# Half of the stack fetches issued by GpSimd, two transfers for the maxima, maxima dealt from the third quad on

## The chip, the cores and the metric

The kernel runs on one core of one Trainium2 chip. The metric is the device time of one execution in microseconds (us). The median of three runs of the kernel before is 1971.94 us (1971.53 to 1973.84).

## The reference

The input `x` has 16 batches of 512 tokens with 256 features. The reference is two residual blocks, each between two layer norms:

```
x = x + layernorm(attention(layernorm(x)))
x = x + layernorm(ffn(layernorm(x)))
```

The attention has 16 heads of 16 features. The 512 tokens are 8 blocks of 64; the first and the last block see all tokens, the others see the first block, the last block and their neighbours:

```
q, k, v = heads(x @ Wq.T + bq), heads(x @ Wk.T + bk), heads(x @ Wv.T + bv)
context = softmax(q @ k.T / 4, over the blocks seen) @ v
```

The second block routes each token to 2 of 8 experts, turns their sum by three matrix exponentials, and mixes it with a dense branch:

```
xn = layernorm(x) * gamma + beta
abel = gelu(xn @ abel_w + abel_b)
moe = sum over the two best of 8 experts of share * (gelu(xn @ w1 + b1) @ w2 + b2)
moe = moe @ expm(g0) @ expm(g1) @ expm(g2)
out = x + abel * (1 - gate) + moe * gate,   gate = sigmoid([abel, moe] @ gc_w + gc_b)
```

## The kernel before

There are three parts one after another: `front` (attention, the dense branch, and the scatter of the tokens to the experts), `experts`, and `last` (gate, norm, residual). The change touches only `front`.

**Steps.** `front` runs 19 steps. Step `s` projects batch `s` (queries, keys, values, and the row maxima of the scores), attends batch `s - 1`, finishes batch `s - 2` (division, norm, residual), and routes batch `s - 3`. Steps 0 to 15 have the projecting part. Each engine has its own program, a list in a fixed order, and waits on semaphores.

**Projection and split.** TensorE projects four blocks `m` = 0 to 3 (L688): queries and keys of heads 0 to 7 (`m` 0 and 1), and of heads 8 to 15 (`m` 2 and 3). Each is split into three bf16 parts that sum to the fp32 value: the first by ScalarE (L914), the rest `resid` by VectorE (L1101), its second part by ScalarE (L922), its third by GpSimd (`third_part`, L1372).

**Stacks.** The scores are then one bf16 product over 96 stacked rows, six combinations of parts for each of the 16 features, so the parts must change partitions. This is done through memory: `put(m)` (L525) stores a split block, 384 KB, in `split_spill`; `restack(m)` (L529) fetches it with six transfers of 128 KB into `qst` or `kst`, 16 partitions and 8 heads of 1 KB rows each. `s_stack[0]` counts the fetches of the first half (`m` 0 and 1), `s_stack[1]` those of the second. All of these are issued by SP, in the order load of `xin` (the input two batches ahead), put 0, put 1, restack 0, put 2, restack 1, put 3, restack 2, restack 3. Behind them come the load of `x1`, the stores of `pre`, the store of `x1`, and the maxima.

**Quads.** The rest of a step goes by 12 quads (`QUADS`), of four units of scores each (L731), with the exponentials on ScalarE (L946) and the product with the values a quad later (L744). Into these TensorE's program deals the 64 row maxima of the projected batch (`max_unit`, L711): unit (h, t) is head h, tile t of 128 rows, into bank `work[t]`, and VectorE reduces it (`maximum`, L1118) and frees the bank. `fill` (L408) deals them evenly over the quads from `B_FROM` = 3 on, counted from 0, so over nine quads. The first waits for `s_stack[0]`, head 8 for `s_stack[1]`. The value projections lie in quads 0 and 1, two turns of the context `turn_ctx` (L761) in quads 1 and 2 behind the third score unit's score, and the dense branch's products (L785) behind quads 2 and 3.

**VectorE's order in a step** (L1237): the rests of the splits and the first two `finish_a` (division of a turned context and its statistics, L1129), `finish_a` 2, the statistics of the next input, `finish_a` 3, the two `values` (the value projection plus its bias, L1110), `ctx_shift`, `x_shift` (both `negated`, L1056), then the maxima of the quads with the routing between them. `ctx_shift` waits for GpSimd's `crstd`, `x_shift` for its `rstd`.

**GpSimd's order in a step** (L1412): four `third_part`, `ln1` (`veps`, `rstd`), the same for the context (`cveps`, `crstd`), the residual, the scatters of `z` (`DMA_INDIRECT`, L1395), and the normed rows `z`.

**Maxima.** `mx` holds column t * 16 + h. It is turned (L724), split in two bf16 parts by ScalarE and VectorE into `mrow` (64 rows of 128), and eight transfers (L597 to L601) write it as two rows of `qst`; the first score unit of the next step waits for them (`s_mrow`).

Of the kernel before, what the change touches and what calls it, by code (L numbers as in the profile page):

```python
# [24 lines left out]
P = 128  # L25
EPS = 1e-5
HEADS, DH, BLK = 16, 16, 64
# [6 lines left out]
NT = len(MEETS)  # L34
# [14 lines left out]
Q_PART = [0, 0, 1, 1, 0, 2]  # L49
K_PART = [0, 1, 0, 1, 2, 0]  # L50
NGRP = len(Q_PART)
# [12 lines left out]
UNITS = HEADS * NCH  # L64
QUADS = UNITS // GROUP
NPB = 8
B_FROM = 3


def tile(ap, t):  # L70
# [72 lines left out]
def wait(eng, s, value):  # L143

    if not isinstance(value, int) or value > 0:
        eng.wait_ge(s, value)


def plain(eng):


    eng.nop(nofuse=True)  # L152
# [59 lines left out]
def front(nc, outer, a, z, kept, w1, w2, b1, b2):  # L212
# [7 lines left out]
    with ctx:  # L220
# [274 lines left out]
        def rot_of(s, par):  # L495
# [3 lines left out]
                return None  # L499
            return "product" if par else "turned"  # L500

        @block.sync
        def _(sp):
            load_x(sp, xin[0], 0, s_xin[0])
# [20 lines left out]
            def put(b, par, m):  # L525
                sp.wait_ge(s_split, b * 4 + m + 1)
                sp.dma_start(spill[par, m], split[:, m, :, :]).then_inc(s_spill[m], 16)

            def restack(b, par, m):  # L529
                half = m // 2  # L530
                st, parts = (kst, K_PART) if m % 2 else (qst, Q_PART)
                sp.wait_ge(s_spill[m], b * 16 + 16)
                for g, part in enumerate(parts):
                    src = spill[par, m].rearrange("(h d) s c -> d h s c", d=DH)[:, :, part, :]

                    sp.dma_start(st[par][g:MASK_ROW:NGRP, 8 * half:8 * half + 8, :], src)\
                      .then_inc(s_stack[half], 16)

            def store_abel(b, par):
                sp.wait_ge(g_abel, b + 1)  # L540
                plain(sp)
# [13 lines left out]

            def step(s, par, i):
                if here(s, 0):
                    if not isinstance(s, int) or s + 2 < B:

                        sp.wait_ge(s_bn, (s + 1) * NTOK)  # L560
                        sp.wait_ge(s_xn, (s + 1) * NTOK)
                        plain(sp)
                        load_x(sp, xin[par], s + 2, s_xin[par])

                    wait(sp, s_sc, (s - 1) * UNITS)
                    plain(sp)
                    if isinstance(s, int) and s < 2:
                        sp.wait_ge(s_rows, 4)
                    put(s, par, 0)
                    put(s, par, 1)  # L570
                    restack(s, par, 0)
                    put(s, par, 2)
                    restack(s, par, 1)
                    put(s, par, 3)
                    restack(s, par, 2)
                    restack(s, par, 3)
                if here(s, 2):
                    b = s - 2

                    wait(sp, g_z, b * NTOK)  # L580
                    plain(sp)
                    wait(sp, s_x1st, b * 16)
                    plain(sp)
                    load_x(sp, x1, b, s_xr)
                if here(s, 4):
                    store_abel(s - 4, par)
                if s_is(s, B + 1):
                    load_w2_behind(2)
                    load_w2_behind(3)
                if here(s, 2):  # L590
                    b = s - 2
                    sp.wait_ge(s_x1, (b + 1) * NTOK)
                    plain(sp)
                    sp.dma_start(kept.of_batches(kept.x1_rows, z)[b], x1[:, :, :]).then_inc(s_x1st, 16)
                if here(s, 0):
                    freed(sp, s, 0, "turn")
                    for t in range(NT):  # L597
                        for part in range(N_MAX):
                            r = MAX_ROW + part
                            sp.dma_start(qst[par][r:r + 1, :, t * P:(t + 1) * P],  # L600
                                         mrow[t * HEADS:(t + 1) * HEADS, part, :]).then_inc(s_mrow, 16)  # L601
                if s_is(s, B):

                    for w in (2, 3):
                        full(sp, B - 1, w, "value")
                    for e in range(2):
                        load_w2(e)
                if s_is(s, B + 1):
                    sp.wait_ge(s_sc, B * UNITS)
                    load_w1(range(NE // 2))  # L610
                    load_w2_behind(4)
                    load_w2_behind(5)
                if s_is(s, B + 2):
                    load_w2_behind(6)
                    load_w2_behind(7)
                    load_w1(range(NE // 2, NE))
# [22 lines left out]
        def _(pe):  # L639
# [91 lines left out]
            def score_unit(b, par, q, n):  # L731

                h, c = q // NCH * GROUP + n, q % NCH
                u = b * UNITS + q * GROUP + n
                if q == 0 and n == 0:
                    pe.wait_ge(s_mrow, (b + 1) * NT * N_MAX * 16)
                wait(pe, s_exp, u - 1)
                for t, at, lo, hi in CHUNKS[c]:
                    ins = nc.tensor.matmul(scT[n % 2][:, at:at + hi - lo],  # L739
                                           tile(kst[par][0:K_EXP, h, :], t),  # L740
                                           qst[par][0:K_EXP, h, lo:hi], start=True, stop=True)
                ins.then_inc(s_sc, 1)
# [163 lines left out]
        def _(act):  # L906
# [18 lines left out]

            def first_max(b):
                full(act, b, 0, "turn")
                wait(act, s_mrow, b * NT * N_MAX * 16)
                nc.scalar.copy(mrow[:, 0, :], work[0][0:NT * HEADS, 0:P]).then_inc(s_m1, 1)

            def norm_x(b, p, j):
# [109 lines left out]
        def _(dve):  # L1041
# [76 lines left out]
            def maximum(b, h, t):  # L1118
                full(dve, b, t, ("max", h))
                n = sum(hi - lo for lo, hi in MEETS[t])  # L1120
                c = t * HEADS + h
                nc.vector.reduce_max(mx[:, c:c + 1], work[t][:, 0:n], AX_X).then_inc(w_free[t], 1)  # L1122

            def second_max(b):
# [4 lines left out]
            def finish_a(b, j):  # L1129

                dve.wait_ge(s_turn, b * NTOK + j + 1)
                tv = turn[:, :].rearrange("p (h e) -> p h e", e=32)
                nc.vector.reciprocal(rden[:, j % 2, :], tv[:, :, DH]).then_inc(s_rden, 1)  # L1133
                dve.wait_ge(s_rden, b * NTOK + j + 1)

                if j == 0:
                    wait(dve, s_x1, b * NTOK)
                inv = rden[:, j % 2, :].rearrange("p (h o) -> p h o", o=1).broadcast_to([P, HEADS, DH])
                nc.vector.tensor_tensor(ctxn[:, j, :].rearrange("p (h d) -> p h d", d=DH),
                                        tv[:, :, 0:DH], inv, ALU.mult).then_inc(s_ctxn, 1)  # L1140
                dve.wait_ge(s_ctxn, b * NTOK + j + 1)
                nc.vector.bn_stats(cstat[:, j, :], ctxn[:, j, :]).then_inc(s_cbn, 1)
                dve.wait_ge(s_cbn, b * NTOK + j + 1)
                plain(dve)
                nc.vector.bn_aggr(cmv[:, j, :], cstat[:, j, :]).then_inc(s_cstat, 1)
# [91 lines left out]
            def step(s, par, i):  # L1237
                proj, finish, routes = here(s, 0), here(s, 2), here(s, 3)
                for m in range(4):

                    if proj:
                        parts(s, m)
                    if finish and m % 2:
                        finish_a(s - 2, m // 2)
                if finish:
                    finish_a(s - 2, 2)
                more = not isinstance(s, int) or s + 1 < B
# [3 lines left out]
                    stats(s + 1, 1 - par)  # L1251
                if finish:
                    finish_a(s - 2, 3)
                if proj:
                    for n in range(2):
                        values(s, par, n)
                if finish:
                    negated(s - 2, s_crstd, cmv[:, :, 0], crstd, cshift, s_cshift)
                if more:
# [98 lines left out]
        def _(pool):  # L1358
# [13 lines left out]
            def third_part(b, m):  # L1372
                pool.wait_ge(s_part2, b * 4 + m + 1)
                nc.gpsimd.tensor_tensor(split[:, m, 2, :], resid[:, m % 2, :], split[:, m, 1, :],  # L1374
                                        ALU.subtract).then_inc(s_split, 1)
# [36 lines left out]
            def step(s, par, i):  # L1412
                if here(s, 0):
                    for m in range(4):
                        third_part(s, m)
                if not isinstance(s, int) or s + 1 < B:
                    ln1(s + 1)
                if here(s, 2):
                    b = s - 2
                    inverse(b, s_cstat, NTOK, cmv[:, :, 1], cveps, s_cveps, crstd, s_crstd)  # L1420
                    residual(b)

                if isinstance(s, int) and s > B and here(s, 2):
                    normed(s - 2, par, i - 1)
                if here(s, 3):
                    scatter(s, s - 3, 1 - par)
                if here(s, 2) and (not isinstance(s, int) or s <= B):
                    normed(s - 2, par, i - 1)
# [547 lines left out]
```

## Time and profile before

| what | value |
|---|---|
| median of 3 runs | 1971.94 us |
| profiled execution | 1979.73 us |
| its span | 1977.9 us |
| mean granted clock of TensorE | 0.942 of full speed |
| TensorE busy | 1598.2 us, 81% |
| VectorE busy | 1217.5 us, 62% |
| ScalarE busy | 930.2 us, 47% |
| GpSimd busy | 706.5 us, 36% |
| fetches from `split_spill` | 384 of 128 KB, median 3.0 us to landing |
| stores to `split_spill` | 64 of 384 KB, median 3.2 us to landing |

The busy times are sums over the three parts; `front` ends a little after 1320 us with its last scatters. A step of `front` repeats every 72 to 76 us, so one step's timeline tells what its 13 equals do. In a timeline a row is a merged run of instructions of one engine; the bracket tells how long the engine was idle before it and what ended that. `SPq` rows are SP's issues of transfers, with the time that the issuing took.

### The profile page before, as it was taken

What the parts mean: (1) busy time and instruction counts of PE and PEld (TensorE: products, weight loads), DVE (VectorE), ACT (ScalarE), POOL (GpSimd) and SP (SyncE); (2) the same over time, 40 slices, a digit from 0 to 9 for tenths busy, and PEclk for the clock granted to TensorE, in tenths of its full rate; (3) what the DMA queues carried; (4) which work ended last, traced back from release to release, by engine and by line L of the source; (5) the groups of instructions that cost most, each with busy time, mean ns of one, the idle gap of its engine ahead of it and who ended that gap; (6) DMA issues with size and microseconds to landing.
All of it is one profiled execution on the core that took longest, in us unless ns stands there. A gap on an engine that the chain in (4) does not pass through costs nothing. (4 is left out here: it accounts for less than half of the span.)

```text
span 1977.9 us, 33425 instructions
## 1 busy us (share of the span) xinstructions
PE 1598.2 (81%) x10429; PEld 1074.0 (54%) x10430; DVE 1217.5 (62%) x3633; ACT 930.2 (47%) x1788; POOL 706.5 (36%) x716
## 2 busy tenths in 40 slices
PE   3888887888888888888888888849999999999800
PEld 2544444444444444444444444538888888888700
DVE  6756675675775775775765765334565566556367
ACT  1045655755755755755755646412332333233234
POOL 1011223423423423423413413522444444444458
PEclk9899999999999999999999998979999999999955
DMA  3233234234234234234144132574565565565377
GB/s 118 80 108 97 67 108 148 74 121 151 73 124 149 70 124 151 72 123 150 68 127 140 60 121 69 165 219 107 124 140 123 114 143 126 108 140 118 45 264 252
DMA packets 185548, 241.47 MB, mean 122 GB/s; under 512 B 24585, under 2 KB 156049, under 8 KB 185297
## 3 DMA queue, kind: packets, MB, share of 16 engines
q1 hardware_dynamic: 158544, 203.58, 32.6%
q0 software_dynamic: 26880, 36.33, 11.1%
q8 instruction: 67, 1.10, 0.2%
q14 instruction: 57, 0.46, 0.1%
HBM read 133.40 MB, written 105.91 MB: 121 GB/s over the span
## 5 line engine op out<-in xcount | busy, mean ns | idle before, releaser
L952 ACT ACTIVATE pexp<-scT 128x512 f32<-128x512 f32 x768 | 441.8, 601 | 355.1 <-PE scT L739 343.8
L1122 DVE TENSOR_REDUCE mx<-work 128x1 f32<-128x320 f32 (+2 forms) x1024 | 492.8, 549 | 50.6 <-PE work L719 47.7
L1599 POOL DMA_INDIRECT y_rows<-rows_add,row_of x144 | 227.0, 1576 | 295.6 <-DMA y_rows<-rows_add,row_of 225.3
L739 PE MATMUL scT<-w 128*128 128x192 bf16 (+3 forms) x1536 | 275.6, 278 | 54.8 <-ACT pexp L952 53.8
L719 PE MATMUL work<-w 126*128 126x320 bf16 (+4 forms) x1280 | 265.8, 300 | 55.4 <-DVE mx L1122 25.9
L1631 PE MATMUL h_ps<-inT,w1c 128*128 128x256 f32 x1152 | 263.1, 382 | 2.4 <-DVE inT L1683 2.4
L1644 PE MATMUL o_ps<-w,hT 128*128 x1152 | 260.4, 379 | 0.0
L1631 PEld LDWEIGHTS h_ps<-inT,w1c 128*128 128x128 f32 x1152 | 220.4, 192 | 33.5 <-issue 2.9
L739 PEld LDWEIGHTS scT<-w 128*128 128x128 bf16 x1536 | 124.3, 98 | 205.4 <-ACT pexp L952 142.0
L1574 ACT ACTIVATE rows_add<-rows_out,row_share 128x257 f32<-128x257 f32 x144 | 65.9, 506 | 354.6 <-DVE rows_out L1699 266.1
L1644 PEld LDWEIGHTS o_ps<-w,hT 128*128 128x128 f32 x1152 | 213.4, 190 | 26.1
L1395 POOL DMA_INDIRECT z_rows<-z,to_row x128 | 125.5, 980 | 225.5 <-DVE to_row L1217 106.7
L719 PEld LDWEIGHTS work<-w 126*128 126x128 bf16 x1280 | 108.5, 98 | 158.7 <-DVE mx L1122 77.4
L1374 POOL TENSOR_TENSOR split<-resid,split 128x512 bf16<-128x512 f32 x64 | 73.4, 1158 | 238.2 <-ACT split L924 238.2
L1692 DVE TENSOR_TENSOR rows_out<-o_ps,b 128x512 f32<-128x512 f32 x72 | 49.8, 692 | 159.1 <-PE o_ps L1644 153.5
L1566 ACT ACTIVATE hT<-h_ps,b1c 128x256 f32<-128x256 f32 x288 | 112.6, 466 | 40.1 <-PE h_ps L1631 40.1
L1382 POOL TENSOR_TENSOR x<-x,ctxn 128x256 f32<-128x256 f32 x64 | 46.4, 728 | 237.7 <-ACT ctxn L943 237.7
L696 PE MATMUL work<-xnT,wqkv 128*128 128x512 f32 x256 | 127.3, 645 | 0.7 <-ACT xnT L912 0.7
L1133 DVE RECIPROCAL rden<-turn 128x16 f32<-128x16 f32 x64 | 15.7, 246 | 158.3 <-PE turn L771 158.3
L1106 DVE SCALAR_TENSOR_TENSOR resid<-work,bqk_sb,split 128x512 f32<-128x512 f32 x64 | 48.0, 750 | 100.3 <-ACT split L919 81.1
L756 PE MATMUL pv<-pexp,b 128*32 128x192 f32 (+3 forms) x1536 | 106.8, 398 | 0.0
L756 PE MATMUL pv<-pexp,vaug 128*32 128x192 f32 (+3 forms) x1536 | 105.5, 394 | 1.2 <-ACT pexp L952 0.9
(173 smaller groups left out, 2176.0 us busy)
## 6 DMA issues: line engine op xcount, KB each, us to landing
w<-split_spill SPq DMA_DIRECT2D x384, 128.0 KB, 3.0
split_spill<-split SPq DMA_DIRECT2D x64, 384.0 KB, 3.2
rows_in<-z_rows SPq DMA_DIRECT2D x72, 265.0 KB, 5.4
y_rows<-pre SPq DMA_DIRECT2D x16, 514.0 KB
y<-y_rows SPq DMA_DIRECT2D x16, 514.0 KB, 6.7
x_rows<-x SPq DMA_DIRECT2D x16, 512.0 KB, 2.6
abel_rows<-pre SPq DMA_DIRECT2D x16, 512.0 KB
abel_in<-abel_rows SPq DMA_DIRECT2D x16, 512.0 KB
```

Source lines behind the costliest of these rows:

```text
L696: ins = nc.tensor.matmul(work[w][:, :], wqkv[:, k, col:col + P], xnT[:, k, :], start=(k == 0), stop=(k == KC - 1))
L719: ins = nc.tensor.matmul(work[t][:, at:at + hi - lo], tile(qst[par][0:K_SCORE, h, :], t), kst[par][0:K_SCORE, h, lo:hi], start=True, stop= ...
L739: ins = nc.tensor.matmul(scT[n % 2][:, at:at + hi - lo], tile(kst[par][0:K_EXP, h, :], t), qst[par][0:K_EXP, h, lo:hi], start=True, stop=True)
L756: ins = nc.tensor.matmul(pv[32 * n:32 * n + 32, lo:hi], vaug[par][:, t, h, :], pexp[:, (q * GROUP + n) % NPB, at:at + hi - lo], start=(c = ...
L952: nc.scalar.activation(pexp[:, (q * GROUP + n) % NPB, :], scT[n % 2][:, :], ACT.Exp, scale=DH ** -0.5).then_inc(s_exp, 1)
L1122: nc.vector.reduce_max(mx[:, c:c + 1], work[t][:, 0:n], AX_X).then_inc(w_free[t], 1)
L1374: nc.gpsimd.tensor_tensor(split[:, m, 2, :], resid[:, m % 2, :], split[:, m, 1, :], ALU.subtract).then_inc(s_split, 1)
L1395: pool.indirect_dma_start(kept.z_rows, bass.IndirectOffsetOnAxis(ap=idx, axis=0), zb[bp][:, j, :], None).then_inc(g_scat[bp], 16)
L1566: nc.scalar.activation(hT[par][:, f, :], h_ps[par][:, f * RT:(f + 1) * RT], ACT.Gelu, bias=b1c[par][:, f:f + 1]).then_inc(e_hT, 1)
L1599: pool.indirect_dma_start(kept.y_rows, bass.IndirectOffsetOnAxis(ap=row_of[n][:, r:r + 1], axis=0), rows_add[n % 2][:, r, :], None, comput ...
L1631: ins = nc.tensor.matmul(h_ps[par][:, f * RT:(f + 1) * RT], w1c[par][:, k, f * P:(f + 1) * P], inT[par][:, k, :], start=(k == 0), stop=(k ...
L1644: ins = nc.tensor.matmul(o_ps[par][:, r * D:(r + 1) * D], hT[par][:, f, r * P:(r + 1) * P], w2[:, bass.ds(e, 1), f, :].rearrange("p o d -> ...
```

## The change

SP issues all four stores first, then the fetches of the first half, and the load of `xin` behind them. GpSimd issues the fetches of the second half, behind its four splits and ahead of `ln1`. The maxima's columns are ordered h * 4 + t, so that two transfers instead of eight carry them. The maxima are dealt over ten quads from quad 2 on. VectorE does `values` ahead of `finish_a` 2.

```diff
-B_FROM = 3
+B_FROM = 2
...
+        def restack(eng, b, par, m):
+            half = m // 2
+            st, parts = (kst, K_PART) if m % 2 else (qst, Q_PART)
+            eng.wait_ge(s_spill[m], b * 16 + 16)
+            for g, part in enumerate(parts):
+                src = spill[par, m].rearrange("(h d) s c -> d h s c", d=DH)[:, :, part, :]
+                eng.dma_start(st[par][g:MASK_ROW:NGRP, 8 * half:8 * half + 8, :], src).then_inc(s_stack[half], 16)
...
             def step(s, par, i):
                 if here(s, 0):
-                    if not isinstance(s, int) or s + 2 < B:
-                        sp.wait_ge(s_bn, (s + 1) * NTOK)
-                        sp.wait_ge(s_xn, (s + 1) * NTOK)
-                        plain(sp)
-                        load_x(sp, xin[par], s + 2, s_xin[par])
                     wait(sp, s_sc, (s - 1) * UNITS)
...
-                    put(s, par, 0)
-                    put(s, par, 1)
-                    restack(s, par, 0)
-                    put(s, par, 2)
-                    restack(s, par, 1)
-                    put(s, par, 3)
-                    restack(s, par, 2)
-                    restack(s, par, 3)
+                    for m in range(4):
+                        put(s, par, m)
+                    for m in range(2):
+                        restack(sp, s, par, m)
+                    if s + 2 < B:
+                        sp.wait_ge(s_bn, (s + 1) * NTOK)
+                        sp.wait_ge(s_xn, (s + 1) * NTOK)
+                        plain(sp)
+                        load_x(sp, xin[par], s + 2, s_xin[par])
...
-                    for t in range(NT):
-                        for part in range(N_MAX):
-                            r = MAX_ROW + part
-                            sp.dma_start(qst[par][r:r + 1, :, t * P:(t + 1) * P],
-                                         mrow[t * HEADS:(t + 1) * HEADS, part, :]).then_inc(s_mrow, 16)
+                    for part in range(N_MAX):
+                        r = MAX_ROW + part
+                        sp.dma_start(qst[par][r:r + 1, :, :].rearrange("o h (t c) -> o (h t) c", c=P),
+                                     mrow[:, part, :]).then_inc(s_mrow, 16)
...
-                    pe.wait_ge(s_mrow, (b + 1) * NT * N_MAX * 16)
+                    pe.wait_ge(s_mrow, (b + 1) * N_MAX * 16)
...
-                wait(act, s_mrow, b * NT * N_MAX * 16)
+                wait(act, s_mrow, b * N_MAX * 16)
...
-                c = t * HEADS + h
+                c = h * NT + t
...
+                if proj:
+                    for n in range(2):
+                        values(s, par, n)
                 if finish:
                     finish_a(s - 2, 2)
...
                 if finish:
                     finish_a(s - 2, 3)
-                if proj:
-                    for n in range(2):
-                        values(s, par, n)
...
                 if here(s, 0):
                     for m in range(4):
                         third_part(s, m)
+                    for m in range(2, 4):
+                        restack(pool, s, par, m)
                 if not isinstance(s, int) or s + 1 < B:
                     ln1(s + 1)
```

## Rows read from the trace of the kernel before

**Rows 1.** The page, its first line and part 1 (busy us, share, instructions).

```profile
span 1977.9 us, 33425 instructions
PE 1598.2 (81%) x10429; PEld 1074.0 (54%) x10430; DVE 1217.5 (62%) x3633; ACT 930.2 (47%) x1788; POOL 706.5 (36%) x716
```

**Rows 2.** Timeline of SP in one step: start us, us of issuing, line, transfer, count.

```profile
753.38 5.03 SPq L600 DMA_DIRECT2D w<-mrow  x8
...
764.23 3.86 SPq L536 DMA_DIRECT2D w<-split_spill  x6
...
768.77 4.70 SPq L536 DMA_DIRECT2D w<-split_spill  x6
...
774.14 7.64 SPq L536 DMA_DIRECT2D w<-split_spill  x12
...
825.55 5.02 SPq L600 DMA_DIRECT2D w<-mrow  x8
```

**Rows 3.** Windows of that step: us, busy us by engine, PEclk, DMA share, GB/s.

```profile
764.90:780.00 15.10, 12.19 (x85) 7.79 (x83) 5.78 (x21) 9.80 (x17) 3.42 (x6) 1.00 0.73 232
780.00:825.50 45.50, 36.23 (x349) 19.43 (x352) 38.50 (x112) 27.76 (x54) 15.94 (x18) 1.00 0.26 87
```

**Rows 4.** The page, part 5: busy us, mean ns, idle before.

```profile
L1122 DVE TENSOR_REDUCE mx<-work 128x1 f32<-128x320 f32 (+2 forms) x1024 | 492.8, 549 | 50.6 <-PE work L719 47.7
```

**Rows 5.** Timeline of VectorE in that step; brackets: idle before, and releaser.

```profile
774.60 0.26 DVE L1133 RECIPROCAL rden<-turn 128x16 f32<-128x16 f32 x1 [8.73 <-PE turn L771]
...
779.09 1.25 DVE L1112 TENSOR_TENSOR b<-work,bv_sb 128x512 f32<-128x512 f32 x2
780.73 0.16 DVE L1059 SCALAR_TENSOR_TENSOR ctx_shift<-cmv,crstd 128x4 f32<-128x4 f32 x1 [0.38 <-POOL crstd L1367]
...
786.97 0.43 DVE L1152 TENSOR_TENSOR pre<-work,bias_ab 128x265 f32<-128x265 f32 x1 [1.25 <-PE work L792]
```

**Rows 6.** Line L1059, what its engine idled for: us in total, times.

```profile
  POOL crstd L1367: 8.4, 16
```

**Rows 7.** Timeline of GpSimd in that step.

```profile
764.21 2.28 POOL L1374 TENSOR_TENSOR split<-resid,split 128x512 bf16<-128x512 f32 x2 [0.56 <-ACT split L924]
778.00 0.23 POOL L1365 TENSOR_SCALAR veps<-mv 128x4 f32<-128x4 f32 x1 [11.52 <-DVE mv L1054]
...
779.66 1.04 POOL L1367 TENSOR_TENSOR crstd<-cveps,neg_half 128x4 f32<-128x4 f32 x1
```

**Rows 8.** The page, part 6: count, KB each, median us from issue to landing.

```profile
w<-split_spill SPq DMA_DIRECT2D x384, 128.0 KB, 3.0
split_spill<-split SPq DMA_DIRECT2D x64, 384.0 KB, 3.2
```

**Rows 9.** GpSimd's transfers: the page, part 5, and a scatter in its timeline.

```profile
L1599 POOL DMA_INDIRECT y_rows<-rows_add,row_of x144 | 227.0, 1576 | 295.6 <-DMA y_rows<-rows_add,row_of 225.3
L1395 POOL DMA_INDIRECT z_rows<-z,to_row x128 | 125.5, 980 | 225.5 <-DVE to_row L1217 106.7
...
811.12 0.96 POOL L1395 DMA_INDIRECT z_rows<-z,to_row  x1 [0.30 <-issue]
```

**Rows 10.** Timeline of GpSimd and VectorE in step 0.

```profile
47.45 2.27 POOL L1374 TENSOR_TENSOR split<-resid,split 128x512 bf16<-128x512 f32 x2 [0.56 <-ACT split L924]
...
51.10 0.16 DVE L1059 SCALAR_TENSOR_TENSOR x_shift<-mv,rstd 128x4 f32<-128x4 f32 x1 [0.39 <-POOL rstd L1367]
```

**Rows 11.** Timeline of GpSimd and VectorE in step 1.

```profile
114.61 2.27 POOL L1374 TENSOR_TENSOR split<-resid,split 128x512 bf16<-128x512 f32 x2 [0.56 <-ACT split L924]
...
127.37 1.55 DVE L1122 TENSOR_REDUCE mx<-work 128x1 f32<-128x320 f32 x3 [4.81 <-PE work L719]
```

**Rows 12.** Timeline of TensorE around the third quad of the step of rows 2.

```profile
776.80 0.39 PE L739 MATMUL scT<-w 128*128 128x192 bf16 x3
...
777.03 0.60 PE L771 MATMUL turn<-ident_sb,ctxT 128*128 128x128 f32 x4
...
781.45 0.80 PE L719 MATMUL work<-w 126*128 126x320 bf16 x3 [1.35 <-DVE pre L1152]
```

More of the change, by code:

```diff
@@ L527, in put @@
                 sp.dma_start(spill[par, m], split[:, m, :, :]).then_inc(s_spill[m], 16)
[L529 to L537, printed above, removed]
             def store_abel(b, par):
@@ L557, in step @@
                 if here(s, 0):
-                    if not isinstance(s, int) or s + 2 < B:
+                    wait(sp, s_sc, (s - 1) * UNITS)
+                    plain(sp)
+                    if isinstance(s, int) and s < 2:
+                        sp.wait_ge(s_rows, 4)
+                    for m in range(4):
[3 more added lines that the diff above has]
+                    if s + 2 < B:
                         sp.wait_ge(s_bn, (s + 1) * NTOK)
@@ L563, in step @@
                         load_x(sp, xin[par], s + 2, s_xin[par])
-                    wait(sp, s_sc, (s - 1) * UNITS)
-                    plain(sp)
-                    if isinstance(s, int) and s < 2:
-                        sp.wait_ge(s_rows, 4)
-                    put(s, par, 0)
-                    put(s, par, 1)
-                    restack(s, par, 0)
-                    put(s, par, 2)
-                    restack(s, par, 1)
-                    put(s, par, 3)
-                    restack(s, par, 2)
-                    restack(s, par, 3)
                 if here(s, 2):
```

## The prediction

> **What bounds the kernel now.** I read the totals first [rows 1]: TensorE is busy 81% of the span, VectorE less, GpSimd 36%, so no engine is full and the question is which waits stand in line. The changed code runs only in the front part, in the 16 steps that project one batch each. SP's own timeline gives the period: the transfers of the maxima start at 753.38 and at 825.55 [rows 2], 72.2 us apart. I follow this step (an even one; odd ones are some 4 us longer and have the same shape).
>
> Two windows of it [rows 3] show two regimes. From 764.9 to 780.0 VectorE works 5.8 of 15.1 us; from 780.0 to 825.5 it works 38.5 of 45.5 us, most of it the row maxima, whose 1024 reductions of 549 ns are the costliest group of the page [rows 4]. So the second stretch is VectorE's: whatever delays its start delays the step. What ends the idle stretch is in VectorE's timeline [rows 5]: it waits 8.73 us for the turn of the context at 774.60, does its statistics, then waits for GpSimd's `crstd` and issues `ctx_shift` at 780.73 (the gate, below), then `pre`, then maxima. That wait stands there 16 times, once per batch [rows 6]. GpSimd is on this path with two short pairs of instructions, from 778.00 to 780.70 [rows 7], and before them it has nothing to do from 766.49 on, 11.5 us. These 11.5 us are what the change fills with 12 transfers.
>
> **Part 1, the 12 fetches on GpSimd.** They stand in GpSimd's program behind the four splits and ahead of ln1 (`rstd`) and of `crstd`, which VectorE waits for, with every maximum queued behind. When can they begin? The third split ends at 764.21 + 1.14 = 765.35, half of the merged row [rows 7]; in the new order SP stores it at once, at 765.4, and a store lands 3.2 us after its issue [rows 8]. GpSimd begins at about 768.7. What does one cost? No row shows a plain transfer issued by GpSimd. The nearest is the scatter of `z`: also 128 rows of about 1 KB, 980 ns mean on the page, 0.96 us with 0.30 us of issue ahead in the timeline [rows 9]. The same rows from SP cost 0.63 us (3.86 for six) [rows 2]. Above is GpSimd's other indirect transfer, 1576 ns [rows 9], 1.88 us with the same 0.30 ahead. Ends: 0.63 and 1.88 us. A plain transfer has no indices to read, so I take the scatter's 0.96 with half of its gap: 1.11 us. Twelve are 13.3 us: done at 782.0. GpSimd should have begun at 778.0. From its 778.00 to the gate are 2.73 us, so the gate moves from 780.73 to 782.1 + 2.7 = 784.9: **+4.2 us a step**. Break-even is (777.9 - 768.7) / 12 = 0.76 us a fetch: below it the fetches are hidden in the idle time. This hits the 14 steps from 2 to 15: 14 x 4.2 = 59 us.
>
> The Trainium skill (DMA: Bandwidth & Descriptors, section Latency and other measured facts) puts the first byte at about 1 us from GpSimd's software path and 0.6 us from SP's. By the skill's figure as an estimate, at 1.0 us a fetch, the gate would move 2.8 us instead of 4.2 and the forecast would come to about 2017 us; the trace agrees as far as it goes, with 0.63 us on SP and 0.96 us for the scatter.
>
> The two first steps have no `crstd`, but `rstd` gates them likewise. In step 0 `x_shift` goes at 51.10, and the whole series for the rotations (20 us of TensorE and VectorE in turns) begins behind it. The third split ends at 48.6 [rows 10], its store lands at 51.9, 13.3 us of fetches end at 65.2, ln1 takes 1.4: 66.7, **+15.6 us**, and nothing else covers it since no attention runs in step 0. In step 1 the third split ends at 115.75 [rows 11], store landed 119.0, fetches to 132.4, `rstd` 133.8, first maximum at about 134.1 where it was 127.37: **+6.7 us**.
>
> **Part 2, SP's order.** The load of `xin` moves behind the fetches; its 2.8 us ended at 761.3, just before the first split was ready, so the first store starts at most 0.2 us sooner. All four stores now come before the first fetch. SP waits for the fourth split (766.49), stores until 767.2, and issues 12 fetches at 0.64: the last is issued at 774.4 and lands 3.0 later [rows 8], at 777.4. Before, the sixth fetch of the pair ended at 773.47 [rows 2], landing near 775.9. The first half thus arrives 1.5 us later. The load of `xin` (wanted a step later), of `x1` and the stores of `pre` have some 15 us to spare: cost 0.
>
> **Part 3, dealing from the third quad on.** The first maxima now stand in TensorE's queue at the third quad behind the score at 776.80, and the turn of the context at 777.03 is queued behind them [rows 12]. They wait for the first half: to 777.4, 0.6 us, up to 2.6 if the two streams slow each other (this stretch has the DMA engines at 0.73 already [rows 3]). With GpSimd late this wait is hidden: `cmv` is ready at 781 at the latest, before 782. What is gained: four maxima stand in the banks when the gate opens, and a quad has 6.4 instead of 7.1. What is lost: the fifth must wait for a bank, and the two dense products, which before ran ahead of the gate (TensorE waited 1.35 us for `pre` at 781.45 [rows 12]), now follow behind six maxima. VectorE's work behind the gate is the same 38.5 us; of its 7.0 us idle there, 1.25 us is one wait for the dense products [rows 5]. Bounds: 1 us lost, 2 us gained. I take 1 us gained a step: 14 x -1 = -14 us.
>
> **Part 4, `values` ahead of the third turn.** 1.25 us leave the tail between the last statistic and the gate, but they lay inside the wait for `crstd` (0.4 us of idle was left). Gain 0; bounds -0.4 and +0.4 a step (the second add now sits just before the reciprocal). **Part 5, two transfers for the maxima.** Six issues go, 5.03 to about 1.3 us of SP. TensorE needs them only at 764.9 and the old eight were issued by 758.4 [rows 2] and landed 1.7 us later, and SP's next work waits for a split. Gain 0, bounds 0 and -0.2.
>
> **Sum.** 59 + 15.6 + 6.7 - 14 = 67 us. On the profiled execution's 1979.73 us (span 1977.9) this is 2047; the median of the runs is 7.8 us lower, so 1971.9 + 67 = **2039 us**.
>
> **Rivals.**
> A, *the cover holds, but TensorE waits at the third quad.* A GpSimd fetch costs 0.63, as SP's, and ends at 776.3. Then the late first half sets the gate: 0.6 to 2.6 us later, less the 1 us of dealing: 14 x (-0.4 to 1.6), plus step 0, where even such fetches end at 59.5 and the series starts 10 us late. 1976 to 2004, say **1990**. For it: DMA engines shared by both streams, already at 0.73. Against it: every GpSimd transfer in the trace costs 0.96 or more. The Trainium skill (DMA: Bandwidth & Descriptors, section Issuing engines are not separate DMA queues) says that issuing on several engines at once saves only the sequencer's time for issuing; by that the two streams bring the data no sooner, which is this case.
>
> B, *the other side: faster.* Fetches under 0.76 us, streams that don't hinder each other, and the dealing takes 2 us out of VectorE's idle time behind the gate: 14 x -2 + 10 = -18, **1954**. Decided by the fetch's price at 0.76 and the first half's landing before about 777. For it: VectorE has 7 us idle behind the gate and 9 ahead of it, and work does move from one to the other. Against it: the gate itself stays.
>
> C, *dear fetches.* 1.88 us each: end at 791.3, gate +13.4, 188 in 14 steps, +25 in step 0, +16 in step 1, -14: **2187**. Against it: that row adds into its target, which this one doesn't.
>
> D, *the fetches don't hold up GpSimd*, because the issue is only handed over. Then nothing but parts 2 and 3 count, without step 0's loss: 14 x (0.6 - 1) = -6, **1966**. Against it: two scatters in a row stand 1.26 us apart, not less [rows 9].
>
> **Chances.** Forecast's mechanism (GpSimd late at the gate, 0.85 to 1.4 us a fetch, 2002 to 2093) 0.66; A 0.13; B 0.10; C 0.04; D 0.07. Inside the forecast's mechanism, 0.96 us a fetch gives 14 x 2.4 + 13.8 + 5 - 14 = +38 (2010), 1.26 gives 14 x 6 + 17.4 + 8.5 - 14 = +96 (2068). The range takes in the half of A and leaves out B, C and the far end: 1982 to 2085. By cases, against the 0.2% (4 us) that measurements of this kernel can tell: faster 0.10 from B and half of D, 0.14 in all; same 0.06 (the rest of D and the low end of A); slower 0.80.
>
> **What would show it.** The price first: GpSimd's rows of the new transfers, twelve per step between its last split and `veps`. Then `veps` at about 15.6 us behind the last split instead of 11.5, VectorE waiting for `crstd` some 3 to 5 us a step instead of 0.5, and `x_shift` of step 0 at 66 instead of 51.1. TensorE should stand still at the third quad, waiting for `mx`. Part 3 is right if VectorE's idle time behind the gate falls by about 1 us. The prediction is wrong if `veps` still follows `mv` at once, or if the fetches cost under 0.76 us; if `turn` at the third quad waits on `split_spill` and GpSimd doesn't, it was A.

## The result and the profile after

| | before | after |
|---|---|---|
| median | 1972.89 us (4 runs) | 2186.16 us (4 runs, 2185.04 to 2190.53) |
| ratio | | 1.107 (95%: 1.1024 to 1.1116) |
| span of the profiled execution | 1977.9 us | 2188.7 us |
| last transfer of the maxima starts at | 1200.5 us | 1416.3 us |
| mean granted clock | 0.942 | 0.896 |

The change costs 213 us, and all of it lies in the 16 projecting steps: the last of them ends with the last transfer of the maxima, which starts 216 us later than before. The forecast was 2039.

The page after, parts 1 and 5 (busy us, mean ns, idle before and releasers). TensorE's group of the maxima, which before idled 55.4 us, idles 222:

```profile
PE 1647.4 (75%) x10429; PEld 1106.6 (51%) x10430; DVE 1226.9 (56%) x3633; ACT 927.1 (42%) x1788; POOL 810.1 (37%) x908
...
L711 PE MATMUL work<-w 126*128 126x320 bf16 (+4 forms) x1280 | 285.3, 314 | 222.2 <-DMA w<-split_spill 133.3
...
L509 POOL DMA_DIRECT2D w<-split_spill x192 | 102.9, 543 | 28.6 <-DMA split_spill<-split 28.5
```

The last row prices what the trace of before could not: a fetch issued by GpSimd costs 0.54 us, about half of the scatter's [rows 9], and 0.06 less than SP's median of 0.60. Its timeline in a step (answers to [rows 7]):

```profile
888.73 2.28 POOL L1366 TENSOR_TENSOR split<-resid,split 128x512 bf16<-128x512 f32 x2 [0.55 <-ACT split L916]
892.47 6.46 POOL L509 DMA_DIRECT2D w<-split_spill  x12 [1.47 <-DMA split_spill<-split]
902.70 0.23 POOL L1357 TENSOR_SCALAR veps<-mv 128x4 f32<-128x4 f32 x1 [3.77 <-DVE mv L1046]
...
915.70 0.23 POOL L1357 TENSOR_SCALAR cveps<-cmv 128x4 f32<-128x4 f32 x1 [11.64 <-DVE cmv L1137]
```

GpSimd is done at 898.93 and then waits for VectorE, 3.77 and 11.64 us. So it is not late. Who is shows in SP's timeline (answers to [rows 2]) and TensorE's (answers to [rows 12]) of the same step:

```profile
879.55 1.17 SPq L592 DMA_DIRECT2D w<-mrow  x2
886.22 5.13 SPq L536 DMA_DIRECT2D split_spill<-split  x4
891.40 8.38 SPq L509 DMA_DIRECT2D w<-split_spill  x12
...
966.90 1.17 SPq L592 DMA_DIRECT2D w<-mrow  x2
```

```profile
900.00 0.39 PE L731 MATMUL scT<-w 128*128 128x192 bf16 x3 [0.47 <-ACT pexp L944]
909.89 0.88 PE L711 MATMUL work<-w 126*128 126x320 bf16 x2 [9.50 <-DMA w<-split_spill]
...
912.97 1.06 PE L763 MATMUL turn<-ident_sb,ctxT 128*128 128x128 f32 x4
...
917.77 0.31 PE L711 MATMUL work<-w 126*128 126x320 bf16 x1 [2.73 <-DVE mx L1114]
...
919.72 3.87 PE L784 MATMUL work<-wab,zT 128*128 128x265 f32 x8 [0.96 <-DVE mx L1114]
```

The step is 87.4 us long, where it was 72.2. TensorE reaches the first maximum at the third quad at 900 and waits there 9.50 us for the first half of the stack, whose last fetch SP issued by 899.78. Behind it in TensorE's queue stands the turn of the context, and behind that, through `cmv` and `crstd`, VectorE's gate. Then TensorE stands a second time, 2.73 and 0.96 us, for banks that VectorE frees only behind the gate. And the two dense products then take 3.87 us, where in the step before the change they took 1.98 and ran ahead of the gate at 780.73:

```profile
777.69 1.98 PE L792 MATMUL work<-wab,zT 128*128 128x265 f32 x8
```

Why the first half is late: windows (answers to [rows 3]) and landings (answers to [rows 8]).

```profile
891.40:900.00 8.60, 6.07 (x38) 3.75 (x38) 1.97 (x4) 5.54 (x10) 6.45 (x12) 1.00 0.94 262
900.00:909.90 9.90, 0.40 (x4) 0.20 (x4) 2.28 (x11) 1.02 (x2) 1.28 (x2) 0.59 1.10 222
909.90:925.00 15.10, 11.12 (x50) 6.12 (x52) 5.45 (x15) 2.14 (x4) 1.26 (x2) 0.61 0.29 87
```

```profile
split_spill<-split SPq DMA_DIRECT2D x64, 384.0 KB, 2.3
w<-split_spill SPq DMA_DIRECT2D x192, 128.0 KB, 6.2
w<-split_spill POOLq DMA_DIRECT2D x192, 128.0 KB, 6.1
```

A fetch from SP took 3.0 us to land, now 6.2, as GpSimd's. The DMA engines go from a share of 0.73 at 232 GB/s to 0.94 at 262 and 1.10 at 222: two issuers, hardly more bytes a microsecond. The bytes of the second half come in place of the first half's. They are not the only ones: the first two windows moved 4.5 MB, and the 24 fetches are 3.1. SP now issues the loads of `xin` and `x` right behind its fetches, from 899.88 on, and then the stores of `pre`; these loads land after 8.1 and 7.4 us here, where they took 2.4 and 2.3 before. The same windows show the clock that TensorE is granted: 1.00, then 0.59 in the stretch in which it stands, and 0.61 in the one after, in which it works again.

One answer to [rows 5] is left: VectorE waits 1.55 us for `crstd` at its gate, where it was 0.38 us. In sum it is 24.8 us where it was 8.4 [rows 6]. The 1.25 us of `values` no longer fill that wait:

```profile
917.08 0.16 DVE L1051 SCALAR_TENSOR_TENSOR ctx_shift<-cmv,crstd 128x4 f32<-128x4 f32 x1 [1.55 <-POOL crstd L1359]
```

### The profile page after: what moved, and what is told of

The parts are those of the page before. It is cut to its first block and busy times, and to the rows that moved or that the text cites. A ratio compares the mean times of both kernels' runs of the same rounds, so it can differ in the third digit from the quotient of the medians.

```text
span 2188.7 us, 33329 instructions
## 1 busy us (share of the span) xinstructions
PE 1647.4 (75%) x10429; PEld 1106.6 (51%) x10430; DVE 1226.9 (56%) x3633; ACT 927.1 (42%) x1788; POOL 810.1 (37%) x908
## 5 line engine op out<-in xcount | busy, mean ns | idle before, releaser
L711 PE MATMUL work<-w 126*128 126x320 bf16 (+4 forms) x1280 | 285.3, 314 | 222.2 <-DMA w<-split_spill 133.3
L731 PE MATMUL scT<-w 128*128 128x192 bf16 (+3 forms) x1536 | 284.9, 286 | 50.8 <-ACT pexp L944 50.1
L711 PEld LDWEIGHTS work<-w 126*128 126x128 bf16 x1280 | 118.9, 101 | 323.8 <-DMA w<-split_spill 136.3
L731 PEld LDWEIGHTS scT<-w 128*128 128x128 bf16 x1536 | 130.1, 101 | 210.1 <-ACT pexp L944 131.5
L688 PE MATMUL work<-xnT,wqkv 128*128 128x512 f32 x256 | 118.1, 606 | 0.7 <-ACT xnT L904 0.7
L748 PE MATMUL pv<-pexp,vaug 128*32 128x192 f32 (+3 forms) x1536 | 112.6, 415 | 1.2 <-ACT pexp L944 0.9
L509 POOL DMA_DIRECT2D w<-split_spill x192 | 102.9, 543 | 28.6 <-DMA split_spill<-split 28.5
```

The source lines that it names most:

```text
L509: eng.dma_start(st[par][g:MASK_ROW:NGRP, 8 * half:8 * half + 8, :], src).then_inc(s_stack[half], 16)
L688: ins = nc.tensor.matmul(work[w][:, :], wqkv[:, k, col:col + P], xnT[:, k, :], start=(k == 0), stop=(k == KC - 1))
L711: ins = nc.tensor.matmul(work[t][:, at:at + hi - lo], tile(qst[par][0:K_SCORE, h, :], t), kst[par][0:K_SCORE, h, lo:hi], start=True, stop= ...
L731: ins = nc.tensor.matmul(scT[n % 2][:, at:at + hi - lo], tile(kst[par][0:K_EXP, h, :], t), qst[par][0:K_EXP, h, lo:hi], start=True, stop=True)
L748: ins = nc.tensor.matmul(pv[32 * n:32 * n + 32, lo:hi], vaug[par][:, t, h, :], pexp[:, (q * GROUP + n) % NPB, at:at + hi - lo], start=(c = ...
```

## The experiments

Two theories for two losses. **S**: the two streams share the DMA engines, the first half lands at half its rate, and TensorE waits for it. **D**: dealing maxima into the third quad costs by itself, since they fill banks that VectorE can free only behind its gate. Rivals: the order of the four stores together with the dealing (P; the order alone is O later), transfers from GpSimd being dear for the DMA engines (H), and GpSimd late at the gate (the prediction's). Each run was timed beside the kernel before on its chip; the ratios are to that.

**All fetches on SP.**

```diff
-                    for m in range(2):
+                    for m in range(4):
                         restack(sp, s, par, m)
...
-                    for m in range(2, 4):
-                        restack(pool, s, par, m)
```

> The changed kernel, but SP issues all 24 fetches, the second half behind the first, and GpSimd none. Theory S (the two streams share the DMA engines, so the first half lands late): the first half has the engines to itself, lands about 13 us after the first fetch's issue less 3, TensorE waits under 1.5 us at the third quad, median 1960 to 1990 us. Rival P (four stores ahead of the fetches, and dealing from the third quad, cost the time by themselves): TensorE still waits 5 us or more a step, above 2080 us.

Measured: 2056.2 us, ratio 1.0387 (1.0336 to 1.0438). The wait on the fetches fell as S said, but only 130 of the 213 us came back:

```profile
PEld work L711 <- DVE mx L1114: 134.8, 194, 3.4
...
PEld work L711 <- DMA w<-split_spill: 24.0, 12, 4.6
```

(The list of waits of this kernel: who waited for what, us in total, times, longest.) Both ranges expected were wrong: a second loss of 82 us remained, and the waits for `mx`, 77.4 us before, were 134.8.

**Dealing from the fourth quad on** (`B_FROM = 3` in the changed kernel).

> The changed kernel, but the maxima are dealt from the fourth quad on (B_FROM = 3). Theory S: the first half lands as late as in the changed kernel, but is wanted a quad and two dense products later, and the turn of the context no longer stands behind it: the wait of 9.5 us a step falls to about 4, median 2070 to 2120 us. Rival P with the dealing as its main part: below 2010 us. Rival of the prediction (GpSimd late at the gate): no wait on the fetches, and crstd late.

Measured: 2056.4 us, 1.0393 (1.0353 to 1.0433). S's range is missed by 14 us, and P's is not reached. TensorE still waits 5.0 us a step for the first half, and these waits are nearly all of the 83 us that remain:

```profile
PE work L711 <- DMA w<-split_spill: 74.9, 15, 9.9
```

**GpSimd's fetches behind `crstd`.**

```diff
-                    for m in range(2, 4):
-                        restack(pool, s, par, m)
                 if not isinstance(s, int) or s + 1 < B:
                     ln1(s + 1)
...
                     inverse(b, s_cstat, NTOK, cmv[:, :, 1], cveps, s_cveps, crstd, s_crstd)
+                if here(s, 0):
+                    for m in range(2, 4):
+                        restack(pool, s, par, m)
```

> The changed kernel, but GpSimd issues its 12 fetches behind crstd instead of ahead of ln1. Theory S: the first half has the engines to itself; the second half is issued some 4 us after the third quad begins, lands within 12 us of that, and is wanted over 15 us after: median 1960 to 1990 us, within 10 us of the kernel with all fetches on SP. Rival H (transfers from GpSimd's queue are dear for the engines whenever they run): the second half takes over 12 us to land and TensorE waits for it at head 8, above 2010 us.

Measured: 2051.4 us, 1.0373 (1.0334 to 1.0412): the same as with all fetches on SP. So it matters when the second half is fetched, not who issues it. S's range is missed here too, by the same second loss. SP's median landing is back at 2.8 us, GpSimd's is 4.7 and TensorE never waits for the second half, so what H expected of the landing falls (its 2010 is passed by the second loss alone). This trace also shows D nearly without S. In this step TensorE waits 0.21 us for the stack (20.4 us in 13 steps) and 3.21 us for a bank:

```profile
827.11 0.53 PE L711 MATMUL work<-w 126*128 126x320 bf16 x2 [0.21 <-DMA w<-split_spill]
...
833.14 0.45 PE L711 MATMUL work<-w 126*128 126x320 bf16 x1 [3.21 <-DVE mx L1114]
...
835.08 3.87 PE L784 MATMUL work<-wab,zT 128*128 128x265 f32 x8 [0.74 <-DVE mx L1114]
```

**Only the fetches on GpSimd, in the kernel before** (its SP order and dealing kept).

```diff
-                    restack(s, par, 2)
-                    restack(s, par, 3)
...
                     for m in range(4):
                         third_part(s, m)
+                    for m in range(2, 4):
...
+                        pool.wait_ge(s_spill[m], s * 16 + 16)
+                        for g, part in enumerate(parts):
...
+                            pool.dma_start(st[par][g:MASK_ROW:NGRP, 8 * half:8 * half + 8, :], src)\
+                              .then_inc(s_stack[half], 16)
```

> The kernel before, and only the second half's fetches moved to GpSimd, behind its splits and ahead of ln1; SP's order of stores and the dealing stay. Theory S: GpSimd's fetches begin when the first half is two thirds fetched, so that it lands 3 to 5 us later than before, near where it is wanted: wait of 0 to 3 us a step, median 1970 to 2015 us. Rival H: the share of the DMA engines per byte rises as in the changed kernel. Rival P: no loss, 1965 to 1980 us.

Measured: 2085.7 us, 1.0529 (1.0478 to 1.0579): both ranges expected were too low (H had none). Here the prediction's mechanism is the one at work. The fourth store is behind twelve fetches in SP's queue, so GpSimd waits for it and is late at the gate, and VectorE waits 4.38 us there (67.1 us in all steps, where it was 8.4):

```profile
772.19 3.29 POOL L1420 DMA_DIRECT2D w<-split_spill  x6 [6.08 <-DMA split_spill<-split]
778.45 3.14 POOL L1420 DMA_DIRECT2D w<-split_spill  x6 [2.96 <-DMA split_spill<-split]
781.61 0.26 POOL L1363 TENSOR_SCALAR veps<-mv 128x4 f32<-128x4 f32 x1
```

```profile
784.37 0.16 DVE L1057 SCALAR_TENSOR_TENSOR ctx_shift<-cmv,crstd 128x4 f32<-128x4 f32 x1 [4.38 <-POOL crstd L1365]
```

**Dealing from the third quad on, in the kernel before** (`B_FROM = 2`, and `values` ahead of `finish_a` 2, no transfer changed).

> The kernel before, with two parts of the change alone: maxima dealt from the third quad on (B_FROM = 2) and values ahead of finish_a 2. All transfers stay with SP in their old order. Theory D (the fifth maximum waits in TensorE's queue for a bank until VectorE passes the gate, and the dense products stand behind it at the lower clock): this alone makes what is left when the streams no longer collide, +4 to +6 us a step, median 2030 to 2060 us. Rival O (the order of stores and fetches makes it): within 10 us of before.

Measured: 2049.1 us, 1.0364 (1.0344 to 1.0384). D holds, O falls: this part alone makes 72 us. In a step TensorE waits for the first half, which it now wants a quad sooner (20.9 us in 12 steps), and then for a bank:

```profile
824.85 0.53 PE L719 MATMUL work<-w 126*128 126x320 bf16 x2 [1.52 <-DMA w<-split_spill]
...
830.88 0.31 PE L719 MATMUL work<-w 126*128 126x320 bf16 x1 [3.22 <-DVE mx L1122]
```

**The two transfers for the maxima, in the kernel before.**

> The kernel before, with the two transfers for the maxima alone (and the columns' order that they need). All theories: the wait for the maxima was 0.5 us in all, so no change, 1965 to 1980 us.

Measured: 1973.7 us, 0.9995 (0.9973 to 1.0017). Nothing.

**Both losses undone** (the changed kernel, GpSimd's fetches behind `crstd` and `B_FROM = 3`).

> The changed kernel with both remedies: GpSimd's fetches behind crstd, and the maxima dealt from the fourth quad on. Theories S and D together: both losses gone, 1965 to 1990 us, equal to before within 1%. If the order of the four stores costs (rival O), above 2000 us.

Measured: 1980.1 us, 1.0014 (0.9998 to 1.0030). As before, with no gain from the rest of the change.

**SP issues all fetches, alternately.**

```diff
                     for m in range(2):
-                        restack(sp, s, par, m)
...
+                        for g, part in enumerate(parts):
+                            for half in range(2):
+                                src = spill[par, 2 * half + m].rearrange("(h d) s c -> d h s c", d=DH)[:, :, part, :]
+                                sp.dma_start(st[par][g:MASK_ROW:NGRP, 8 * half:8 * half + 8, :], src)\
+                                  .then_inc(s_stack[half], 16)
```

> The changed kernel, but SP issues all 24 fetches alternately, one of the first half, one of the second; GpSimd none. Theory S in its plain form (the first half is late because the second takes every other place, whoever issues it): as late as in the changed kernel, TensorE waits 8 us or more at the third quad, median 2150 to 2200 us, though the share of the DMA engines stays near 0.75. Rival H (GpSimd's queue makes the packets dearer): the first half lands with SP's issue rate, 15.2 us for 24, and the wait is 3 us or more shorter than in the changed kernel, 2090 to 2140 us.

Measured: 2197.8 us, 1.1118 (1.1096 to 1.1139): at least as slow as the changed kernel, with no transfer of the stack on GpSimd. TensorE waits 141.9 us in 15 steps. In a step:

```profile
899.82 16.02 SPq L570 DMA_DIRECT2D w<-split_spill  x24
...
917.33 0.87 PE L718 MATMUL work<-w 126*128 126x320 bf16 x2 [8.12 <-DMA w<-split_spill]
```

```profile
899.80:909.00 9.20, 7.71 (x40) 4.60 (x40) 2.12 (x5) 4.88 (x10) 0.00 (x0) 0.81 0.59 184
909.00:917.30 8.30, 0.21 (x3) 0.01 (x1) 2.13 (x10) 0.84 (x2) 1.27 (x2) 0.67 0.69 205
```

H falls as the cause: the first half is late without GpSimd's queue. The share of the engines is only 0.59 to 0.69 here, so what binds is SP's 0.67 us an issue; in the changed kernel it is the engines. Here the first half is complete 17.5 us after the first issue, there 18.5, since its last fetch is the last but one of 24 or shares with all of them.

But GpSimd's packets do take longer, as H has it. Part 3 of the pages gives, for each queue, its packets, its MB, and the time that its packets took as a share of the 16 engines' span. First the kernel with all fetches on SP (span 2054.2 us), then the one with GpSimd's fetches behind `crstd` (2049.3 us):

```profile
q1 hardware_dynamic: 157008, 203.57, 30.5%
q0 software_dynamic: 26880, 36.33, 10.6%
...
q1 hardware_dynamic: 129360, 178.40, 26.8%
q0 software_dynamic: 36096, 61.51, 15.8%
```

The second half's 25.2 MB take 77 us of each engine's time when SP issues them (the shares times the spans, subtracted) and 106 us when GpSimd does, over a third more. How much of the changed kernel's wait that makes is not shown. These times may hold what packets waited for each other as well.

**`values` ahead, alone.**

> The kernel before, with values ahead of finish_a 2 alone. Theory D and all others: they lay inside the wait for crstd, so no change, 1965 to 1985 us; if this is above 2010 us, the loss of the kernel with both was not the dealing's.

Measured: 1983.4 us, 1.0023 (1.0005 to 1.0042): some 4 us, at the edge of what can be told. So of the 72 us some 66 are the dealing's.

**Four maxima in the third quad**, one for each bank (in the kernel with `values` ahead, as is the next).

```diff
+            if q == B_FROM - 1:
+                return [[], units[0:2], units[2:4], []][n]
+            units = units[4:]
```

> The kernel before, with values ahead, and in the third quad only four maxima, one in each bank (head 0, tiles 0 to 3); the other 60 over nine quads as before. It asks what TensorE waits for. Theory D1 (the dense products 0 and 1 need banks 0 and 1, which four maxima fill until VectorE passes the gate, so they no longer run ahead of it): no fifth maximum, but TensorE stops at the dense products instead, loss of 2 us or more a step, 2005 to 2050 us. Theory D2 (it is the fifth and sixth maximum that stop TensorE): without them no loss, 1960 to 1985 us.

Measured: 2030.0 us, 1.0255 (1.0217 to 1.0293). D1: over two thirds of the loss remain without a fifth maximum, and the fifth and sixth make the other 19 us. TensorE stops at the dense products, which before ran ahead of the gate, and they take nearly twice the time:

```profile
896.20 3.55 PE L795 MATMUL work<-wab,zT 128*128 128x265 f32 x8 [3.31 <-DVE mx L1125]
```

**Two maxima in the third quad**, in banks 2 and 3.

```diff
+            if q == B_FROM - 1:
+                return [(0, n + 1)] if n in (1, 2) else []
+            units = [u for u in units if u not in ((0, 2), (0, 3))]
...
-                if t == 0 and h % 8 == 0:
+                if (h, t) in ((0, 2), (8, 0)):
```

> As the one with four maxima in the third quad, but only the two whose banks the dense products do not need (head 0, tiles 2 and 3); the other 62 over nine quads. Theory D1: the dense products run ahead of the gate again, no stop in the third quad, and two maxima wait ready for VectorE: loss gone, 1955 to 1980 us, perhaps 0.3% under before. Theory D2: the same. If dealing anything into the third quad costs by itself (the wait for the first half of the stack ahead of the turn of the context), above 1995 us.

Measured: 2005.0 us, 1.0134 (1.0100 to 1.0169). Both D1 and D2 expected no loss; the third case did come, that dealing anything there costs by itself. It is 22 us above the kernel with `values` alone. The dense products are ahead of the gate again (1.98 us), but VectorE now reduces two maxima before `pre`, and TensorE waits longer for `pre` at the fourth quad, 1.99 us where it was 1.35 [rows 12]; and it waits 21.4 us in 12 steps for the first half, now ahead of the turn (3.1 us with `values` alone):

```profile
879.88 1.98 PE L795 MATMUL work<-wab,zT 128*128 128x265 f32 x8
...
884.27 0.73 PE L722 MATMUL work<-w 126*128 126x320 bf16 x2 [1.99 <-DVE pre L1155]
```

**GpSimd waits for the first half before it fetches the second**, still ahead of `ln1`.

```diff
+                    pool.wait_ge(s_stack[0], (s + 1) * 2 * NGRP * 16)
                     for m in range(2, 4):
                         restack(pool, s, par, m)
```

> The changed kernel, but GpSimd waits for the first half to have landed before it issues the second, still ahead of ln1. Theory S: the first half lands as early as with GpSimd's fetches behind crstd, TensorE's wait on it falls from 9 us to under 1.5; but now the mechanism that the prediction put first comes in: first half landed at the third quad, 6.4 us of issuing, so crstd is 5 to 7 us late. Against the kernel with the fetches behind crstd (2051) that is 5 x 14 = 70 us or more: 2110 to 2160 us. If the wait for GpSimd cost nothing, 2050 us.

Measured: 2131.8 us, 1.0777 (1.0741 to 1.0813), 80 us above the same fetches behind `crstd`, as expected. In the step shown TensorE's wait on the first half is 1.17 us, and GpSimd is what is late:

```profile
881.33 6.46 POOL L509 DMA_DIRECT2D w<-split_spill  x12 [10.78 <-DMA w<-split_spill]
887.82 0.26 POOL L1357 TENSOR_SCALAR veps<-mv 128x4 f32<-128x4 f32 x1
```

```profile
890.58 0.16 DVE L1051 SCALAR_TENSOR_TENSOR ctx_shift<-cmv,crstd 128x4 f32<-128x4 f32 x1 [5.70 <-POOL crstd L1359]
```

Put together, four kernels that differ in two things only (us, and ratio to before):

| | second half fetched behind `crstd` | together with the first |
|---|---|---|
| maxima from the fourth quad on | 1980, 1.0014 | 2056, 1.0393 |
| from the third quad on | 2051, 1.0373 | 2186, 1.107 |

The collision alone costs 76 us, the dealing alone 71, and both 206: some 60 more than the sum. The dealing puts the first maxima, and behind them the turn of the context, a quad nearer to the late stack. TensorE's waits for the stack are 2.5, 74.9, 20.4 and 133.3 us in the four, in the order of the table, so they rise by 40 us more together than apart; where the other 20 lie was not looked for.

## Why the prediction was wrong

The direction was right; the size was off by a factor of three, and the mechanism put first was not the one at work. That rival C stood at 2187, by the measured time, is chance: its fetch of 1.88 us was 0.54. By the prediction's own sign (the third quad waits on `split_spill` and GpSimd is not late) it was A.

- *Part 1, the price of a fetch.* 1.11 us was taken, between 0.63 and 1.88; measured is 0.54, below both ends. Twelve take 6.5 us, not 13.3, and end inside GpSimd's idle time. The second estimate, at 1.0 us a fetch, took a time to the first byte for the time that an issue holds its engine; the 0.63 and 0.96 us that it called agreement are times of the second kind. The break-even of 0.76 us held in this order of SP. So the +4.2 us a step at the gate were 0 (VectorE's wait there rose from 0.38 to 1.55 us, by the 1.25 us of `values` that went ahead). GpSimd's mechanism itself is real where the fetches start late: in two experiments it cost 112 and 80 us.
- *Part 3, the wait for the first half.* This is the step that failed. It was written as 0.6 us, up to 2.6 "if the two streams slow each other"; measured is 133.3 us in 15 steps, 8.9 each. The reading of SP's rows was the error: 0.63 us per 128 KB is 208 GB/s, and the window's 232 GB/s at a share of 0.73 leaves, as an estimate, 318 GB/s for full engines, where two such streams ask for 416. They got less still, 222 to 262; GpSimd's longer packets may be why, but that was not tested. Twelve more fetches at GpSimd's rate mean 3.1 MB before the first half is complete, at 222 to 262 GB/s 12 to 14 us from 891.4, plus some 3 us for the last to land. It took 18.5; the loads behind SP's fetches share that stretch, and whether they are the other 1 to 3 us was not tested. Rival A named this and priced it at 1990.
- *Part 3, the dealing.* -1 us a step was taken, bounds +1 and -2. Measured are +72 us, 4.8 a step, of which `values` are some 4 us in all. The prediction saw that "the fifth must wait for a bank" and that the dense products now follow behind the gate, but set this off against VectorE's gain. Of the 66 us above the kernel with `values` alone, 22 are there with two maxima outside the dense products' banks (TensorE's wait for the first half rises by 18 in that run); 25 more come with the dense products' banks filled, whose products then take 3.55 us for 1.98; the fifth and sixth maximum make 19.
- *The clock* had no term. It was granted at 1.00 where TensorE before waited 1.35 us; behind the 9.50 us it is 0.61.
- *Step 0 and 1.* +15.6 and +6.7 were taken. The maxima of step 0 go at 114.15 where it was 105.31, +8.8, and step 1 takes 74.2 us from there where it took 63.6, +10.6. In step 0 `x_shift` waits 7.15 us for `rstd` and goes at 60.36, not 66.7, by the cheaper fetch: this is the mechanism as told. The 14 steps behind have the other 196 us, 14.0 each.
- *Parts 2, 4 and 5* were right as far as they were tested: SP's order and the two transfers cost nothing that can be measured (1.0014 with both in and GpSimd's fetches late, 0.9995 for the transfers alone), `values` some 4 us. What the loads behind the fetches cost while GpSimd's run too was not tested.

## What to carry to other kernels

Before a second engine issues transfers beside the first, divide the first one's bytes by its issue time: where the two rates together are more than the DMA engines move, the second stream takes its bandwidth from the first, and the transfer that is wanted first comes in late. Order transfers by when they are wanted, and start those with slack behind the ones without. And work that is moved ahead of a gate also takes the banks of what already ran ahead of it: count what then stands behind.

## What the runs showed of the hardware

- A plain transfer of 128 rows of 1 KB costs GpSimd 0.54 us with no gap between two, SP 0.60 to 0.67; the indirect one of as many rows 0.96 and a gap of 0.30. The Trainium skill (DMA: Bandwidth & Descriptors, section Latency and other measured facts) has about 1 us to the first byte for GpSimd's path and 0.6 for SP's; that is another quantity, and it didn't carry over to the issuing engine's time.
- Two streams of such fetches raise their landing from 3.0 to 6.2 us at nearly the same total (232 GB/s before, 262 and 222 after). The Trainium skill's sentence that DMAs from several engines run on the same 16 DMA engines and interleave (DMA: Bandwidth & Descriptors, section Issuing engines are not separate DMA queues) is what the runs show, with its price here: 76 us with the maxima from the fourth quad on, 130 to 135 from the third.
- The same 25.2 MB took 77 us of each DMA engine's time when SP issued them and 106 us when GpSimd did (two different runs, of 2054.2 and 2049.3 us).
- After 9.50 us of waiting TensorE gets a clock of 0.61 in the next 15 us, against 1.00 before: between its two levels (1.2 and 2.4 GHz) for parts of the stretch; the same eight matmuls take 3.87 instead of 1.98 us. After 3.21 us of waiting at a bank they take 3.87 us as well (granted clock 0.65 from 832.4 to 842.0).
